# Scan layer: the first convolution tap of chunks 1 to 3 moves from VectorE to ScalarE

## The reference

```
xz = layernorm(x) @ in_proj_w.T          # 2*1024 rows, 256 -> 1024
x, z = split(xz)                         # 512 channels each
xc = depthwise causal conv of x, 4 taps, + conv_b
x = silu(xc)
dt, B, C = split(x @ x_proj_w.T);  dt = softplus(dt @ dt_proj_w.T + dt_proj_b)
h = exp(dt * A) * h + dt * B * x         # over time, for 16 states
y = sum over states of h * C + x * D
out = x_in + (y * silu(z)) @ out_proj_w.T
```

## Time and profile before

| what | value |
|---|---|
| time, median of 3 runs | 1749.55 us (1747.53 to 1751.8) |
| the profiled execution | 1751.08 us |
| its span, first to last instruction | 1749.3 us |
| PE busy | 1474.2 us (84%) |
| DVE busy | 1048.4 us (60%) |
| ACT busy | 892.5 us (51%) |
| POOL busy | 947.0 us (54%) |
| `times_c` L878 on POOL, 256 of them | 322.5 us |
| `scan` L786 on DVE, 2 x 128 | 152.3 + 157.4 us |
| `times_b` L604 and `decay` L614 on ACT, 256 each | 181.7 + 181.6 us |

### The profile page before, as it was taken

The page is one execution under the profiler, slowest core; times in us unless marked ns, Lnnn a source line. Parts: engine busy times, 40 slices in busy tenths (PEclk is TensorE's granted clock), DMA queues, the critical chain, the costliest instruction groups (busy, mean ns, idle before and its releaser), DMA issues. The chain is left out here.

```text
span 1749.3 us, 29587 instructions
## 1 busy us (share of the span) xinstructions
PE 1474.2 (84%) x10646; PEld 1222.4 (70%) x10646; DVE 1048.4 (60%) x2026; ACT 892.5 (51%) x1585; POOL 947.0 (54%) x763
## 2 busy tenths in 40 slices
PE   5887888899977876984989997985794999999993
PEld 1566567577854665982668887973683888888883
DVE  6777878779967864536775454458737432322224
ACT  4897798799934643643712235535443422223230
POOL 0599699799936834962021135030533638593871
PEclk8899999999988996996989998988885999999997
DMA  3000101011021026513000000030034512242144
GB/s 137 16 35 25 49 26 49 25 50 49 26 78 35 2 92 230 195 64 125 2 1 25 1 1 1 1 91 8 2 97 185 158 50 102 83 145 79 58 154 165
DMA packets 54075, 118.81 MB, mean 68 GB/s; under 512 B 14070, under 2 KB 34940, under 8 KB 46512
## 3 DMA queue, kind: packets, MB, share of 16 engines
q1 hardware_dynamic: 45200, 84.00, 13.8%
q0 software_dynamic: 8576, 32.91, 5.6%
q10 hardware_dynamic: 160, 0.02, 0.0%
HBM read 92.41 MB, written 24.43 MB: 67 GB/s over the span
## 5 line engine op out<-in xcount | busy, mean ns | idle before, releaser
L878 POOL TENSOR_TENSOR HC<-H,CB 128x512 f32<-128x512 f32 x256 | 322.5, 1296 | 77.2 <-DVE H L786 63.3
L604 ACT ACTIVATE UT<-DTXT,BT 128x512 f32<-128x512 f32 x256 | 181.7, 712 | 28.1 <-PE ps L452 27.6
L452 PE MATMUL ps<-ident,UT 128*128 128x128 f32 x1024 | 165.9, 287 | 28.5 <-DVE H L786 16.6
L452 PEld LDWEIGHTS ps<-ident,UT 128*128 128x128 f32 x1024 | 123.5, 147 | 90.1 <-DVE H L786 41.1
L614 ACT ACTIVATE dA<-DT,nA 128x512 f32<-128x512 f32 x256 | 181.6, 711 | 3.3 <-DVE H L786 3.2
L786 DVE TENSOR_TENSOR_SCAN H<-dA,ps 128x512 f32<-128x512 f32 x128 | 152.3, 1212 | 45.1 <-PE ps L452 34.6
L786 DVE TENSOR_TENSOR_SCAN H<-dA,HL,ps 128x512 f32<-128x512 f32 x128 | 157.4, 1267 | 25.7 <-PE ps L452 17.5
L461 PE MATMUL ps<-ident,HC 128*128 128x128 f32 x1024 | 157.8, 282 | 12.2 <-POOL HC L878 10.5
L2323 DVE TENSOR_TENSOR f_XN<-f_XN,ps 128x1024 f32<-128x1024 f32 x39 | 47.6, 1221 | 153.7 <-PE ps L160 153.7
L461 PEld LDWEIGHTS ps<-ident,HC 128*128 128x128 f32 x1024 | 122.6, 146 | 19.9 <-POOL HC L878 19.5
L158 PE MATMUL ps<-f_W,f_DIT 128*128 x312 | 128.0, 410 | 1.7 <-issue 1.7
(11 more groups left out here) (628 smaller groups left out, 4148.6 us busy)
## 6 DMA issues: line engine op xcount, KB each, us to landing
CB<-m_c_rows SPq DMA_DIRECT2D x16, 1024.0 KB, 4.5
f_w<-in_f_w SPq DMA_DIRECT2D x16, 1024.0 KB, 5.1
f_stage<-in_f_w POOLq DMA_DIRECT2D x15, 1024.0 KB, 5.1
f_stage<-in_f_w SPq DMA_DIRECT2D x9, 1024.0 KB, 6.8
f_xn_rows<-f_XN SPq DMA_DIRECT2D x8, 512.0 KB, 12.2
f_W<-f_y_rows SPq DMA_DIRECT2D x4, 1024.0 KB, 8.8
f_rows_in<-f_DI SPq DMA_DIRECT2D x23, 128.0 KB, 2.0
f_DI<-f_rows_in SPq DMA_DIRECT2D x23, 128.0 KB, 2.2
```

The source lines that it names most:

```text
L452: ins = pe.transpose(PS[4 + G % UR][:, t * P:(t + 1) * P], UT[:, n % 2, t, c * P:(c + 1) * P], g.ident[:, :])
L604: act.activation(UT[:, N % 2, t, :], DTXT[:, k % 2, t, :], ACT.Copy, scale=BT[:, k % 2, t, n:n + 1]).then_inc(ut_ready, 1)
L878: pool.tensor_tensor(HC[:, y, :], H[:, s, :], CB[:, n // 4 % CR, n % 4, :], ALU.mult).then_inc(hc_ready, 1)
```

## The change

`first_tap` takes the chunk as well, and ACT now does tap 0 for chunks 1 to 3 too, in its loop, after its steps 6, 7, 11 and 13 for blocks 0 to 3. On DVE tap 0 is gone, and tap 1 waits for ACT's tap (`tap_ready`) in all chunks. DVE's own order is otherwise the same.

```
-                def first_tap(c):
-                    act.wait_ge(in_full, c + 1)
-                    act.activation(DT[:, 0, c, :], PS[6 + c % 2][:, :], ACT.Identity, bias=conv_b[:, c:c + 1],
+                def first_tap(k, c):
+                    act.wait_ge(in_full, k * CI + c + 1)
+                    act.activation(DT[:, k % 2, c, :], PS[6 + c % 2][:, :], ACT.Identity, bias=conv_b[:, c:c + 1],
                                    scale=conv_w[:, c, DC - 1:DC]).then_inc(tap_ready, 1)
...
                             for j in at((0, 0), p):
                                 keep_columns(k + 1, j)
+                            for c in at((6, 7, 11, 13), p):
+                                first_tap(k + 1, c)
                             for c in at((15, 15, 15, 15), p):
                                 silu_x(k + 1, c)
...
-                    if j == 0 and k == 0:
+                    if j == 0:
                         return
-                    if j == 0:
-                        dve.wait_ge(in_full, k * CI + c + 1)
-                        ch.add(dve.tensor_scalar(o, x[:, :], w, conv_b[:, c:c + 1], ALU.mult, ALU.add))
-                        return
-                    if j == 1 and k == 0:
-                        dve.wait_ge(tap_ready, c + 1)
+                    if j == 1:
+                        dve.wait_ge(tap_ready, k * CI + c + 1)
```

More of the change, by code:

```diff
@@ L622, in _ @@
                 act.wait_ge(loaded_small, 16 * 6)
-                first_tap(0)
+                first_tap(0, 0)
                 for c in range(1, CI):
-                    first_tap(c)
+                    first_tap(0, c)
                     silu_x(0, c - 1)
```

## The result

The changed kernel took 1757.71 us (median of 6 executions, 1755.51 to 1763.8), against 1749.66 us (6 executions, 1747.53 to 1751.8) before: a ratio of 1.0055, 95% interval 1.004 to 1.007. It is slower by 8 us. Run again later it gave 1.0071 (1.0055 to 1.0087). Slower is clear of noise; its size lies between 7 and 15 us, and single executions of one kernel spread over up to 13 us.

The account below looks back on a forecast made before the run. DVE was taken to bound each chunk's convolution stretch and POOL the rest. Lateness of 6.4 us plus 1.5 us for one clock fall, 7.9 us on the median 1749.55, gave 1757.4 us, range 1751.5 to 1763.

Parts of the forecast that it names:

- main term: Sum over chunks 0 to 2 of DVE's lateness at block 3's tap: 6.4 us later.
- The sign that it named: In the trace after, the three scans behind the convolution come 2.7, 4.4, then 6.4 us later in sum, clock apart.
- What bounds it: DVE sets the pace in each chunk's convolution stretch, POOL in the rest; a DVE delay is handed on.
- Block 0's tap: ACT's queue delays it, so DVE's tap 1 starts 2.54, 1.86 and 1.92 us late in chunks 0, 1 and 2.
- Blocks 1 and 2: Removing each tap gives DVE 0.71 us back; block 1's is ready in time, block 2's readiness hardly matters.
- Block 3's tap: Late through PE and ACT's queue: DVE's tap 1 2.67, 1.71 and 2.02 us late in chunks 0 to 2, replacing earlier lateness.
- b: Lateness of scan 5 after block 1's tap: 1.83, 1.15 and 1.21 us in chunks 0, 1 and 2.
- The clock: PE's clock falls in gaps while DVE waits for ACT; one more fall taken, 1.5 us.
- the upper bound: Five more clock falls, two behind the convolution and three at block-0 waits: 7.5 us, giving 1763.5 us; 1761 or more 13%.
- The errata table: Estimate of 0.57 us for ACT's tap where the trace shows 0.78; the sum would be 5.1 us; not used.
- The gain: Rival: ACT's taps are in time and DVE loses 8.5 us of work, giving 1741 us; chance 6%.
- The absorption by POOL's ring: Rival: DVE's lateness only shortens its 5.62 us wait for POOL's full ring, 1749.5 us; chance 16%, halves included.

Follow-up runs that it names:

- e1: The changed kernel again, unaltered, giving its second profile: 1761.06 us.
- e7: Against the changed kernel, only block 0's first tap on ACT (step 6), the other three on DVE again: 1755.85 us, 1.0034 of the kernel before.
- e8: Against the changed kernel, only block 3's first tap on ACT (step 13), the other three on DVE again: 1755.82 us, 1.0032 of the kernel before.
- e2: The changed kernel with block 3's tap behind ACT's step 11 instead of 13: 1749.98 us, 1.0007 of the kernel before.
- e3: The changed kernel with the four taps behind ACT's steps 3, 5, 10 and 11 instead of 6, 7, 11 and 13: 1746.89 us.
- e5: The changed kernel with 12 unused identity transposes added behind each of PE's steps 13 and 14 in chunks 0 to 2: 1762.54 us.

## Why the prediction was right, point by point

**The time.** Forecast 1757.4 us, measured 1757.71, in the range of 1751.5 to 1763. The agreement to 0.3 us is luck: two profiles of the same program are 6.9 us apart (spans 1753.7 and 1760.6). What it can claim is the sign and the size of its main term. The sign that it named shows both: scan 13 of chunks 0, 1 and 2 should come 2.7, 4.4 and 6.4 us later, clock apart, and came 2.8, 4.4 and 7.3 us later in e1, with 3.6, 7.8 and 10.3 in the first profile, where the clock had fallen in chunk 0.

**What bounds it.** DVE in the convolution stretch and POOL behind it: right. The lateness was handed on: from scan 18 to the next chunk, chunk 2 took 77.7 to 78.0 us in nine profiles at the same granted clock (0.96), with DVE between 2.0 us early and 1.8 us late at scan 13, and chunk 0 took 81.5 to 81.7 us in all profiles but one.

**Block 0's tap.** Forecast 2.54, 1.86 and 1.92 us late. e7 alone measured 2.5, 1.75 and 1.8 us at scan 13. The size is a little high, since 0.88 us from ACT's start to DVE's was too long: 62.44 - 61.65 = 0.79 and 186.49 - 185.69 = 0.80 us in the loop, where the tap took 0.76 us and not 0.78.

**Blocks 1 and 2** are in time: right; no waits for them are among the six. Block 1's 0.71 us came back at scan 13, block 2's was lost in the wait for block 3's tap, as the sum had it.

**Block 3's tap.** Late by b, through PE, and by its own place in ACT's queue: right, and the point on which the sum hangs. What it replaces is only DVE's own lateness behind block 2; block 0's lateness is inside b, and its loss and block 3's add up (e7 and e8). Forecast 2.67, 1.71, 2.02 us, sum 6.4; measured in e1 2.55, 1.57, 1.84, sum 6.0; in the first profile 3.68, 1.57, 1.85, of which 1.1 us in chunk 0 are the clock. e2 removes this wait and the loss; e8 has it alone, at the size that the same counting gives.

**The clock.** Right in kind, and its place was right, but the term was undersized. I took one more fall at 1.5 us. The first profile had no more slow stretches than the kernel before, one against one, and the second had two. To scan 18, the changed kernel lost 2.1 us by the clock in the first profile (1.1 in chunk 0's convolution, 26.92 - 25.96 = 0.96 behind it) and 3.3 in the second. A fall behind the new wait costs 2.5 us (10.6 - 8.1), not the 1.5 that chunk 2 of the kernel before had shown: an estimate from PEclk 0.69 over 10.65 us and 0.82 over 9.70 us is that 6.6 us of the slow stretch were at 1.2 GHz, against 3.5. The step that was off is taking the price of a fall from a place with less idle time: PE had gaps of 0.24 and 1.86 us there, and of 1.74 and 1.86 us in chunk 0 of the changed kernel. The falls at the block-0 waits, which the upper bound priced at 1.5 us each, did come, three in the first profile and two in the second, and cost 1.1 us in chunk 0 and nothing in chunk 2; in chunk 1 no profile of these kernels is without one, but the distance there is within 0.2 us of the forecast that has none. What made up for it in the first profile were the layers behind, 6.0 us shorter (1238.2 to 1232.2), which no step of mine had; in the second they were 3.2 us longer.

**The errata table** (the Trainium skill, "VectorE: DVE Perf Modes", section on the TRN2 errata). The estimate of 0.57 us for a tap that I worked out from it is not borne out: 0.76 us in the new ones shown above, and 0.66 us from such a tap's start to the start of ACT's next instruction.

**The rivals.** The gain did not arrive, and by the reason given, ACT's position: moved to steps 3, 5, 10 and 11 the same taps are in time (e3). The absorption by POOL's ring did not happen: the stretches behind scan 18 have the same length whether DVE comes early or late (see above).

**Still open.** How often the clock falls in a stretch and what that is in the median. Filling the gaps removes the falls behind the convolution in every profile, and the medians of the changed kernel and of e8 don't drop. The falls may move to places where one profile per kernel doesn't show how often they happen. The 4 us by which e8 is slower than its waits account for are therefore shown as falls in its profile, and not in its median; for the median their cause is open. The same holds for the 2 to 6 us by which the changed kernel's medians exceed the 6.0 us of its waits.

## What to carry to other kernels

When work moves to an engine that has idle time, ask at which place of its queue the idle time lies. Here ACT was idle 28% of the stretch, and the late taps stood in the other 72%; the same four instructions at steps 3, 5, 10 and 11 make the kernel 2 to 3 us faster than before, and at 6, 7, 11 and 13 slower by 8 to 12. Put a moved instruction ahead of the wait that the queue has anyway, not behind it: an engine that would idle there anyway loses next to nothing (e2). And an instruction that runs while its engine waits for something else, like block 0's tap before scan 4, is free: moving it gains nothing.

Before summing late arrivals, ask what carries one to the next. Here block 0's lateness reached block 3 through PE, so the two losses added up, while time saved on DVE behind the last such link was swallowed by the next wait. And when two parts are run alone and compared with the whole, count everything else that the whole contains.

## What the runs showed of the hardware

The same instructions from scan 13 to 18 take 8.1 to 8.4 us with PEclk at 1.00, 9.6 to 9.9 us at 0.82 or 0.83 and 10.5 to 10.7 at 0.68 or 0.69. Useless transposes in the two gaps, 12 and 12 or 4 and 12 of them, went with PEclk at 1.00 in 15 stretches of 15; without them it was 1.00 in 17 of 27. A fall is not always paid for: in chunk 2, up to scan 13, PEclk 0.94 (e1) and 1.00 (e5) gave the same 31.75 us.

I had not expected how much of a kernel's spread the clock goes with. Layers in which the instructions are identical took 1232.2 to 1246.4 us in fourteen profiles, with PEclk 0.92 in the two shortest and 0.91 in the longest, against a loss of 8 us that was to be explained. With such a spread the distances to scan 13 in chunks 1 and 2, which repeat to 0.1 us, tell causes apart, and a median over 4 to 12 executions doesn't where they are worth 2 or 3 us.
